# Masking the attention scores with signed copies of the adjacency, and turning the probabilities per query tile

## What is computed

```python
h = relu(layernorm(x)); x = x + L0(h, adj)   # (adj @ h) -> 256x1024 -> RMS norm, SiLU -> 1024x256
h = relu(layernorm(x)); x = x + L1(h, adj, nodemask)  # sigmoid(s1_i + s2_j) * adj, rows normalised
h = relu(layernorm(x)); x = x + L2(h, adj, adj)
h = relu(layernorm(x)); x = x + L3(h, adj)   # d^-1/2 adj d^-1/2 @ h @ W + b

def L2(h, edge, adj_mask):                   # 8 heads of 32
    scores = q @ k.T / sqrt(HD) + W_e[head] * edge
    scores = where(adj_mask, scores, -inf)
    return softmax(scores) @ v @ W_o.T
```

## Time and profile before

| | us |
|---|---|
| median of 3 runs | 3797.84 (3796.89 to 3798.93) |
| the profiled execution | 3793.83 |
| its span | 3792.0 |
| TensorE busy | 3595.9 (95%) |
| VectorE busy | 2623.7 (69%) |
| ScalarE busy | 2279.2 (60%) |
| GpSimd busy | 772.2 (20%) |
| TensorE in the chain that ended last | 61% of the span |

### The profile page before, as it was taken

One profiled execution on the slowest core, in us unless ns is written; L12 is line 12 of the kernel. 1 busy time (PEld: TensorE's weight loads), 2 busy tenths in 40 slices (PEclk: granted clock), 3 DMA queues, 4 the chain that ended last, 5 costly groups with the idle time before them and its releaser, 6 DMA issues.

```text
span 3792.0 us, 67268 instructions
## 1 busy us (share of the span) xinstructions
PE 3595.9 (95%) x19375; PEld 2445.7 (64%) x19596; DVE 2623.7 (69%) x6436; ACT 2279.2 (60%) x5029; POOL 772.2 (20%) x1611
## 2 busy tenths in 40 slices
PE   4899999999999999999999999999999999999997
PEld 3566666666666666666666666666666666666664
DVE  4676776666767766767767766667677667677664
ACT  2565666555666656666656665556666566666564
POOL 1122211222212222212222112222122222122210
PEclk9999999999999999999999999999999999999999
DMA  2232132322232322223321323222323222233212
GB/s 85 62 85 72 56 89 56 89 74 69 67 78 67 89 67 67 78 57 87 85 71 56 89 56 89 75 70 67 78 67 89 67 67 78 57 87 85 65 45 67
DMA packets 166936, 275.09 MB, mean 73 GB/s; under 512 B 23906, under 2 KB 59874, under 8 KB 166756
## 3 DMA queue, kind: packets, MB, share of 16 engines
q1 hardware_dynamic: 166756, 273.45, 26.7%
HBM read 122.37 MB, written 16.78 MB: 37 GB/s over the span
## 4 chain that ended last, share of the span: by engine, by line
PE 61%; issue 13%; DVE 12%; POOL 8%; ACT 5%; POOLq 0%; DMA 0%; DVEq 0%; SPq 0%; another core or an unknown queue 0%; ACTq 0%
PE turn L1213 9%; PE front L1026 7%; PE score L1203 6%; PE front L1027 6%; PE front L1028 6%; PE score L1204 4%; PE value L1228 3%; POOL small L374 3%; PE front L1056 3%; PE front L1079 3%; PE score L1177 3%; PE value L1189 3%; DVE pT L813 2%; ACT hf L500 2%; PE front L1068 2%
## 5 line engine op out<-in xcount | busy, mean ns | idle before, releaser
L588 ACT ACTIVATE prob<-prob,small 128x512 f32<-128x512 f32 x1024 | 736.1, 719 | 375.4 <-DVE small L888 373.8
L888 DVE CUSTOM_DVE_ANT_0 prob<-score,adj_sb,drv 128x512 f32<-128x512 f32 x1024 | 759.4, 747 | 224.8 <-PE score L1204 126.9
L1213 PE MATMUL turn<-ident,prob 128*128 128x128 f32 x4096 | 617.1, 276 | 14.6 <-ACT pT L597 8.7
L1213 PEld LDWEIGHTS turn<-ident,prob 128*128 128x128 f32 x4096 | 484.9, 141 | 134.8 <-issue 62.0
L597 ACT ACTIVATE pT<-turn 128x512 f32<-128x512 f32 x768 | 446.5, 584 | 144.6 <-PE turn L1213 144.6
L1203 PE MATMUL score<-qk_stack 128*128 128x512 f32 x1024 | 496.0, 488 | 31.5 <-DVE small L888 29.9
L1026 PE MATMUL front<-w_hi,s_hi 128*128 128x256 f32 x1024 | 353.0, 345 | 28.6 <-DVE x_in L792 28.6
L1204 PE MATMUL score<-unlinked,neg_mask 128*128 128x512 bf16 x803 | 313.6, 391 | 0.0
L680 DVE TENSOR_TENSOR s_lo<-front,s_hi 128x512 fp32r<-128x512 f32 x320 | 217.7, 680 | 102.7 <-ACT s_hi L486 102.6
L1027 PE MATMUL front<-w_lo,s_hi 128*128 128x256 f32 x1024 | 288.0, 281 | 0.0
L1028 PE MATMUL front<-w_hi,s_lo 128*128 128x256 f32 x1024 | 287.6, 281 | 0.0
(11 more groups left out here) (160 smaller groups left out, 7447.2 us busy)
## 6 DMA issues: line engine op xcount, KB each, us to landing
qk_stack<-qk SPq DMA_DIRECT2D x1024, 128.0 KB, 2.4
adjT_f<-in_adjT SPq DMA_DIRECT2D x32, 1024.0 KB, 5.0
adj_sb<-in_adj SPq DMA_DIRECT2D x32, 1024.0 KB, 7.9
prob<-in_adjT SPq DMA_DIRECT2D x32, 1024.0 KB, 5.4
x_new<-in_x SPq DMA_DIRECT2D x32, 512.0 KB, 3.7
out<-x_out SPq DMA_DIRECT2D x32, 512.0 KB, 3.1
pT<-in_W SPq DMA_DIRECT2D x2, 1024.0 KB
rmsw_b<-in_rmsw SPq DMA_DIRECT2D x1, 512.0 KB
```

The lines of the kernel that those rows point to most:

```text
L588: act.activation(prob[:, i % 8, :], prob[:, i % 8, :], ACT.Exp, bias=nmax[:, h, n:n + 1], scale=-1.0, accum_out=prsum[:, h, n:n + 1]).then ...
L888: dve.tensor_tensor_reduce(out=prob[:, i % 8, :], in0=SB_[i % 2][:, :], in1=adj_sb[:, n, :], scale=neg_w[:, h:h + 1], scalar=3e38, op0=ALU ...
L1213: last = pe.transpose(TB[k % 2][:, tile(n)], prob[:, (4 * h + n) % 8, tile(j)], ident[:, :])
```

## The change

**The mask.** Instead of `unlinked`, VectorE makes two versions of the adjacency in the tensor `edges`, for the graph of the next round: `edges_neg` is the adjacency plus 1e37 where there is no edge, and in the place of the adjacency stands the adjacency minus 1e37 there (twice itself minus the first). `far_nodes`, `edges_below` and `edges_above` write them. For each score tile GpSimd copies one of the two, by the sign of the head's weight (`below`, read into registers at the start), to one of three slots of `edge` (`pick_edges`); the bias takes it from there. The mask matmul is gone. The degree sum (`degree`) moves from the start of the round to the end of the one before.

**The turns.** A turn takes one query tile of one head, all four key tiles, and needs one exp. The probabilities have four slots, `pT` five head buffers; `x_new` lies over the fifth, so the load of x waits for the last `attend`. In step g stand score and bias g + 4, exp g + 3, turn g + 2 and copy g + 1. The front half's pieces move by two steps, `tanh`, `silu` and the parts each by a step against each other, the last tile's quarters go to two steps, and there is one step fewer.

**Around it.** `aggregate(nx, 1)` and what follows it move from the end of a round to the start of the next, behind the q and k projections, which now use the turn banks; the second values' projection goes into step -3. The fourth bank of `project3` is FB[2]. The stack has three slots. The diff, cut to its core:

```diff
-        neg_mask = sb("neg_mask", [P, H, P], BF16)
+        below = sb("below", [P, H], mybir.dt.int32)
...
-        adj_sb = sb("adj_sb", [P, NT, N])
-        unlinked = sb("unlinked", [P, NT, N], BF16)
+        edges = sb("edges", [P, 2, NT, N])
+        adj_sb, edges_neg = edges[:, 0, :, :], edges[:, 1, :, :]
+        edge = sb("edge", [P, 3, N])
...
-        qk_stack = sb("qk_stack", [P, 4, 2, N], F32R)
+        qk_stack = sb("qk_stack", [P, 3, 2, N], F32R)
...
-        prob = sb("prob", [P, 8, N])
-        adjT_b = prob[:, 0:NT, :]
-        pT = sb("pT", [P, HG, NT, N])
+        prob = sb("prob", [P, NT, N])
+        adjT_b = prob[:, :, :]
+        pT = sb("pT", [P, HG + 1, NT, N])
+        x_new = sb("x_new", [P, NT, D], over="pT", skip=4 * HG * NT * N)
...
-            return [(n, g + 4 - 8 * n) for n in range(NT) if 0 <= g + 4 - 8 * n < 16]
+            return [(n, g + 6 - 8 * n) for n in range(NT) if 0 <= g + 6 - 8 * n < 16]
...
-                return range(4) if u == 8 else ()
-            return (u - 11,) if 11 <= u < 15 else ()
-
-        GRID = range(-4, 4 * H)
-        Q1_STEP, K1_STEP = 0, 3
+                return (2 * u - 20, 2 * u - 19) if u in (10, 11) else ()
+            return (u - 10,) if 10 <= u < 14 else ()
+
+        def update_step(n):
+
+            return 12 if n == NT - 1 else 14
+
+        GRID = range(-4, 4 * H - 1)
+        Q1_STEP, K1_STEP = 1, 4
...
+            def pick_edges(t, i):
+
+                h, n = divmod(i, NT)
+                if h == 0:
+                    pool.wait_ge(edges_ready, at(t, 4, n + 1))
+                if i >= 3:
+                    pool.wait_ge(biased, at(t, 32, i - 2))
+                elif later(t):
+                    pool.wait_ge(out_ready, at(t, 4, 0))
+                unregistered(pool)
+                pool.tensor_copy(edge[:, i % 3, :], edges[:, bass.ds(sign_of[h], 1), n, :].rearrange("p o n -> p (o n)")).then_inc(edge_picked, 1)
...
-                            elif u in (6, 7):
-                                hidden_hi(tf, n, u - 6)
-                    if b and g + 4 < 4 * H:
-                        exps(t, g + 4)
-                    if b and g >= 0 and g % 4 != DVE_TURN:
-                        turned_probs(t, g // 4, g % 4)
+                            elif u in (7, 8):
+                                hidden_hi(tf, n, u - 7)
+                    if b and g >= -1 and (g + 1) % NT != DVE_TURN:
+                        turned_probs(t, g + 1)
+                    if b and 0 <= g + 3 < 4 * H:
+                        exps(t, g + 3)
+                    if b and g == -2:
+                        values(t, 1)
...
-                dve.tensor_scalar(unlinked[:, :, :], adj_sb[:, :, :], 0.0, None, ALU.is_equal).then_inc(unlinked_ready, 1)
-                dve.tensor_reduce(deg, adj_sb[:, :, :], AX.X, ALU.add).then_inc(deg_ready, 1)
...
+            def far_nodes(tf):
+
+                dve.tensor_scalar(edges_neg, adj_sb, 0.0, BIG, ALU.is_equal, ALU.mult).then_inc(far, 1)
+
+            def edges_below(tf):
+
+                dve.wait_ge(far, at(tf, 1, 1))
+                for n in range(NT):
+                    dve.tensor_tensor(edges_neg[:, n, :], adj_sb[:, n, :], edges_neg[:, n, :], ALU.add).then_inc(edges_neg_ready, 1)
+
+            def edges_above(tf):
+
+                dve.wait_ge(deg_ready, at(tf, 1, 1))
+                for n in range(NT):
+                    dve.wait_ge(edges_neg_ready, at(tf, 4, n + 1))
+                    dve.scalar_tensor_tensor(out=adj_sb[:, n, :], in0=adj_sb[:, n, :], scalar=2.0, in1=edges_neg[:, n, :],
+                                             op0=ALU.mult, op1=ALU.subtract).then_inc(edges_ready, 1)
...
-                if n == 0 and h >= 2:
-
-                    dve.wait_ge(b_turned, at(t, N_turned, turn_of_prob[h - 2, NT - 1] + 1))
+                if i >= NT:
+
+                    dve.wait_ge(b_turned, at(t, N_turned, turn_of_prob[i - NT] + 1))
+                dve.wait_ge(edge_picked, at(t, 32, i + 1))
                 unregistered(dve)
-                dve.tensor_tensor_reduce(out=prob[:, i % 8, :], in0=SB_[i % 2][:, :], in1=adj_sb[:, n, :],
+                dve.tensor_tensor_reduce(out=prob[:, i % NT, :], in0=SB_[i % 2][:, :], in1=edge[:, i % 3, :],
...
-                pe.matmul(SB_[i % 2][:, :], qk_stack[:, h % 4, 0, tile(n)], qk_stack[:, h % 4, 1, :], start=True, stop=False)
-                pe.matmul(SB_[i % 2][:, :], neg_mask[:, h, :], unlinked[:, n, :],
-                          start=False, stop=True).then_inc(sc_ps, 1)
...
+                pe.matmul(SB_[i % 2][:, :], qk_stack[:, s, 0, tile(n)], qk_stack[:, s, 1, :], start=True, stop=True).then_inc(sc_ps, 1)
+
+            def turn_probs(t, i):
+                pe.wait_ge(exped, at(t, 32, i + 1))
+                k = turn_of_prob[i]
+                wait_bank(t, k)
+                for j in range(NT):
+                    last = pe.transpose(TB[k % 2][:, tile(j)], prob[:, i % NT, tile(j)], ident[:, :])
+                last.then_inc(b_turned, 1)
```

273 lines of the change are left out of this document (144 added, 129 removed).

## The result

The changed kernel takes **3826.56 us** (median of 4 runs, 3824.06 to 3828.17) against 3797.36 for the kernel before (4 runs, 3795.54 to 3798.93): ratio 1.0076, 95% interval 1.0059 to 1.0094. It is slower by 0.8%; the forecast was 2% faster.

The account below looks back on a forecast made before the run. TensorE, busy 111.6 of 115.07 us a batch, was taken as the bound. Mask 7.4 off, waits from 3.5 to 8.8: 113.0 a batch; 31 batches and the last one's 7 give 3722 profiled, 3725 median; range 3600 to 3840.

Parts of the forecast that it names:

- the port: Rival: GpSimd's pick holds VectorE's silu in the head steps through the shared SBUF port; 87 us in all, 3812; chance 0.07.
- GpSimd's pace: Rival: GpSimd's picks pace the light head steps, 1.39 us a pick, 4.4 us a batch on top: 3863; chance 0.13.
- Part 1: Head steps: dropping the mask matmul takes 32 x 0.23 us, 7.4 us a batch, off TensorE.
- turn's 1.0: Ahead of `turn`: `far_nodes` on the way to the layernorm makes TensorE wait 1.0 us a batch.
- part 4: Turns per query tile, one step behind exp: waits of 2.45 us at the start, 0.2 between, 2.3 in the last tile.
- six light steps in a row: Steps of a tile where ScalarE is not covered by TensorE, though over all eight it needs about 12.0 against 12.5 us.
- Part 2: VectorE's two signed copies: `far_nodes` costs 1.0 us a batch ahead of `turn`; `edges_below` and `edges_above` nothing, 2 at most.
- Part 3: GpSimd's 32 picks a batch in the head steps, 0.7 us each, are hidden and cost nothing.
- Part 5: End of the head steps: chain from last quarter to last spread 7.5 us; TensorE waits 2.4 there in place of 0.4.
- Part 6: Stack slots, fifth head buffer and `x_new` over it: the later load of x (3.7 us) costs nothing.
- The gain is eaten up: Rival: waits grow by 7.4 us a batch, in the chain of light steps: 3790, within 0.2%; chance 0.05.
- The feeders keep up: Rival: most mid-step waits do not show, 6.0 us of waits, 110.2 us a batch: 3637; chance 0.22.

Follow-up runs that it names:

- after_fill_both: Changed kernel with small matmuls that nothing reads at both places where TensorE idles, the first head steps and the spread of s1: 3793 us.
- after_lag: Changed kernel without GpSimd's picks, a fifth probability slot letting each turn come one step later: 3811.9 us against 3822.8 without picks alone.
- the square: Four runs, old or new turns with old or new tile steps, `edges_below` apart: new tile steps cost 112 us with new turns, 428 with old.
- after_offset4: Changed kernel with `edges_below` behind `update3`, tiles two steps later against scores and turns, the new order inside a step kept: 3879.5 us.

## Why the prediction was wrong

Forecast: a period of 113.0 us, 3722 for the profiled execution. Measured: 116.0 and 3827. The difference, 3.0 us a batch, is 1.2 (mask), 1.7 (clock) and 0.1 (waits); 31 x 3.0 = 93, and 9 us of the first front half; the last 3 are the last batch (1) and rounding. The step that failed is the one from waits to time: the sum charged new waits at their own length and the clock at nothing. Without the clock's 53 us the kernel would stand, by this account, near 3774, faster than before by 0.6%. The measured 3826.6 lies within the stated 3600 to 3840, but by luck: the range reached so high for the port's 3812 and a part of GpSimd's pace, costs that did not occur.

- **Part 1, the mask, mis-sized: 7.4 forecast, 6.2 measured** (5.6 and 6.6 in the two runs on it). Step by step (score to score, waits taken out, the kernel before with and without the mask) 0.23 us is right in 18 of 31. Most of the others, the steps with turned hidden tiles among them, get only 0.01 to 0.18 shorter: I multiplied a row from a full step by 32.
- **The clock, missing: 1.7 us a batch.** The prediction named it only as what would make it wrong. It had itself found some 5 us of waits in two clusters, 2.45 at the first turns and 2.4 before the spread, and the falls stand behind just these. That they hang on the idle pieces is shown by `after_fill_both`.
- **Waits: size right, cause wrong.** Start 2.45 forecast, 2.73 measured; last tile 2.3 and 2.15; before the spread 2.4 and 1.9; the tiles between 0.2 and 1.8 (1.3 where k's projection stands ahead and 0.5 for a low part; none in the tile with the attend pieces); turn's 1.0 shows as 0.3, within `turn`; small ones 0.45 and 0.4; together 8.8 and 8.94. That the sums agree is partly luck: 1.6 too little between the tiles makes up for 0.5 and 1.0 too much elsewhere. And I laid all of part 4's waits on the one step between exp and turn. `after_lag` shows that this step is not what makes them, the square and `after_offset4` that the order inside the tile steps is. The prediction had priced the bare steps (1.1 us for TensorE, 1.7 for ScalarE) and "six light steps in a row", but took them as given and never asked where the quarters stood before.
- **Part 2, wrong in its mechanism.** I priced `far_nodes` as time in VectorE's queue and `edges_below` at nothing. What counts is whom they hold: GpSimd's small steps. The prediction used the port rule in one direction only, GpSimd's pick against VectorE's silu. There it is harmless: silu's median is 0.69 us, as before, and its longest 0.82, where the prediction expected over 1; it was the pick that was held (median 0.61, mean 0.72, longest 1.09).
- **Part 3 right**: pick 0.61 us undisturbed, hidden.
- **Part 5 right in the length of its chain**: from the last down matmul to the last spread 7.6 us (7.5 forecast). **Part 6 right**: the load of x takes 5.7 us and nobody waits.
- **The ends**: the last batch 6.1 us less (7 forecast). That the first front half, with nothing beside it, would take 8.8 us longer was in no term. The square has it from both: the new tile steps make "first" 7.1 us longer with the old turns (125.0 to 132.1) and 3.7 with the new, the new turns and the moves with them 5.9 and 2.5.
- **The rivals**: none came out. The shared port's 3812 was nearest in time, with the effect the wrong way round: it had GpSimd hold VectorE's silu. "The gain is eaten up" (3790) had the right kind of loss, but not the clock. "The feeders keep up" argued that "the present steps have no wait in their middle". That says only that TensorE was slow enough: without the mask the same steps have 2.7 us more of waits. Two sums of this part are off without weight: it gives 3639, not 3637, and by its own numbers (0.07 between two picks, 1.24 us a light step) GpSimd would pace from a pick of 1.17, not 1.28.

## What to carry to other kernels

When the bounding engine gets faster, list its steps with each feeder's time in the same step, before and after: the sums may be equal and the pairing be lost, and that was 112 us here against 3 for moving the turns. Where the bounding engine is TensorE, a new idle piece can cost twice, for itself and for the clock behind it: look at the granted clock, and at every such place before mending one. Taking the longest idle pieces away brought more here than filling them: 3716 to 3636 us, and fills on top of that nothing measurable. And ask of each operation added to an engine with slack whom it holds: VectorE had 28 us a batch to spare, the four small GpSimd steps beside it had none.

## What was not expected of the hardware

- Useless matmuls in idle pieces made the kernel faster: 12 a batch, -34 us. Filling one of two places, with 4, made it slower by 27 us: the fall of the clock came at the other place in every batch, and the 4 matmuls were only partly hidden.
- A GpSimd step of 128x4, 0.20 us, took 2.43 us beside four VectorE sums of 128x512 with both operands in SBUF, and 1.09 beside one `tensor_scalar` of 128x2048 in float32; beside sums with one operand in PSUM a step kept its time (1.02 us).
- GpSimd's copy of 128x512 float32 takes 0.61 us (median), less than half of its two-input sum (1.39).
